# Four graph layers in one kernel: edge sums copied to a second half of the partitions, gate bias moved from products into bias columns

## The reference

```
# layer 1 (gated): means of neighbours, then a GRU cell
feat_in, feat_out = h @ W_in.T + b_in, h @ W_out.T + b_out
a  = concat(mean of feat_in[src] by dst, mean of feat_out[dst] by src)
gi, gh = a @ w_ih.T + b_ih, h @ w_hh.T + b_hh
r = sigmoid(i_r + h_r); z = sigmoid(i_z + h_z); n = tanh(i_n + r * h_n)
h = (1 - z) * n + z * h
# layer 2 (MLP): edge attributes summed per node
agg = segment_sum(edge_attr, col)                 # 3125 x 64
h = concat([x, agg, u[batch]])                    # 128 + 64 + 64 wide
h = leaky_relu(h @ w1 + b1); h = leaky_relu(h @ w2 + b2); out = h @ w3 + b3
```

## Time and profile before

| | |
|---|---|
| median of three runs | 860.36 us |
| profiled execution | 858.32 us, of which the span from first to last instruction is 856.6 us |
| busy share of the span | TensorE products 93%, weight loads 82%, DVE 71%, ACT 38%, GpSimd 3% |
| chain that ended last | PE 86%, DVE 8%, ACT 2%, issue 2%, DMA 1% |
| mean granted TensorE clock | 0.963 |

### The profile page before, as it was taken

How to read it: one execution, slowest core, us unless ns; L and a number is a source line. 1 busy time by engine, 2 the same in 40 slices (tenths; PEclk the granted TensorE clock), 3 DMA queues, 4 the chain that set the end, 5 groups by cost and what they waited for, 6 DMA issues and landing times.

```text
span 856.6 us, 16030 instructions
## 1 busy us (share of the span) xinstructions
PE 797.1 (93%) x6347; PEld 705.9 (82%) x6347; DVE 611.3 (71%) x970; ACT 324.6 (38%) x579; POOL 21.6 (3%) x39
## 2 busy tenths in 40 slices
PE   5699999999989999999989999979987999999995
PEld 2599999999979999789989996434546999699994
DVE  6998999999968777687876774657467455035654
ACT  0243444454556222522453332263325332432233
POOL 3500000000000000000000000000000000000000
PEclk9577999999998999999999999999999999999998
DMA  5455788888850000000000000000000000000001
GB/s 107 99 125 116 158 188 176 180 182 176 177 111 21 1 1 2 1 1 1 1 19 1 1 1 3 0 13 0 1 0 26 0 0 1 1 1 1 1 25 52
DMA packets 161175, 42.16 MB, mean 49 GB/s; under 512 B 155049, under 2 KB 159666, under 8 KB 161094
## 3 DMA queue, kind: packets, MB, share of 16 engines
q1 hardware_dynamic: 147882, 38.97, 20.3%
q10 hardware_dynamic: 11932, 0.81, 1.0%
q0 software_dynamic: 1280, 1.29, 0.6%
HBM read 39.04 MB, written 2.01 MB: 48 GB/s over the span
## 4 chain that ended last, share of the span: by engine, by line
PE 86%; DVE 8%; ACT 2%; issue 2%; DMA 1%; SPq 0%; POOL 0%; DVEq 0%; ACTq 0%
PE bank L1674 20%; PE bank L1675 19%; PE bank L1612 15%; PE bank L1602 10%; PE bank L1878 2%; PE bank L1810 2%; PE bank L1867 2%; PE bank L1866 1%; PE bank L1886 1%; PE bank L1736 1%; PE bank L1929 1%; PE bank L1930 1%; PE bank L1687 1%; DVE stage L1106 1%; PE bank L1814 1%
## 5 line engine op out<-in xcount | busy, mean ns | idle before, releaser
L1674 PE MATMUL bank<-stage,f_hi 125*128 125x392 f32 x1000 | 347.2, 347 | 3.8 <-issue 2.3
L1675 PE MATMUL bank<-stage,f_lo 125*128 125x392 f32 x1000 | 341.0, 341 | 0.0
L1106 DVE CAST stage<-counts 125x2352 fp32r<-125x2352 uint8 x120 | 164.2, 1380 | 77.0 <-PE bank L1675 76.9
L768 ACT ACTIVATE stage<-counts 125x1568 fp32r<-125x1568 uint8 x80 | 108.1, 1351 | 227.2 <-PE bank L1675 224.9
L1674 PEld LDWEIGHTS bank<-stage,f_hi 125*128 125x128 f32 x1000 | 188.7, 189 | 5.7 <-issue 4.0
L1675 PEld LDWEIGHTS bank<-stage,f_lo 125*128 125x128 f32 x1000 | 188.6, 189 | 0.6
L1612 PE MATMUL bank<-tmp,wb 128*65 128x25 f32 x2000 | 135.4, 223 | 0.2 <-DVE tmp L1064 0.2
L1612 PEld LDWEIGHTS bank<-tmp,wb 128*65 128x65 f32 x2000 | 132.1, 147 | 0.8 <-DVE tmp L1064 0.5
L722 ACT ACTIVATE counts<-bank 125x500 uint8<-125x500 f32 x188 | 87.9, 536 | 47.7 <-PE bank L1602 46.6
L1602 PE MATMUL bank<-rowb,xT 128*128 128x125 bf16 x1250 | 90.1, 230 | 10.0 <-DVE rowb L1042 5.3
L1039 DVE TENSOR_TENSOR xT<-xT,tmp 128x2560 bf16<-128x2560 bf16 (+1 forms) x63 | 92.8, 1473 | 2.5 <-PE bank L1602 2.4
(11 more groups left out here) (217 smaller groups left out, 674.8 us busy)
## 6 DMA issues: line engine op xcount, KB each, us to landing
wb<-in_edge_attr SPq DMA_DIRECT2D x125, 256.0 KB, 3.9
wa<-in_x SPq DMA_DIRECT2D x12, 125.0 KB
out<-wl SPq DMA_DIRECT2D x6, 250.0 KB
xT<-in_dst SPq DMA_DIRECT2D x63, 4.0 KB, 3.5
xT<-in_dst ACTq DMA_DIRECT2D x62, 4.0 KB, 3.2
wb<-in_L_gnn_w_ih SPq DMA_DIRECT2D x1, 384.0 KB, 3.4
gate_w_d<-wl SPq DMA_DIRECT2D x1, 384.0 KB, 4.2
counts<-in_dst SPq DMA_DIRECT2D x1, 360.9 KB
```

Source lines behind the costliest of these rows:

```text
L768: nc.scalar.activation(set_buffer(u, m), counts[:, SETS[u][0]:sum(SETS[u]), chunk(c)], ACT.Copy).then_inc(s["set_a_ready"], 1)
L1106: nc.vector.tensor_copy(set_buffer(u, m), counts[:, SETS[u][0]:sum(SETS[u]), chunk(pair * 2 + off)]).then_inc(s["set_d_ready"], 1)
L1674: mm(bank[h][:, 0:CH], f_hi[:, first + k, :], rhs[:, k, :], start=(first + k == 0), stop=False)
L1675: last = mm(bank[h][:, 0:CH], f_lo[:, first + k, :], rhs[:, k, :], start=False, stop=(first + k == HI - 1))
```

## The change

`hidden1` now issues the two products with `xT` first and then the two 64-row products, the second of which reads its weights (`l2w1b`) and its edge sums from partitions 64 to 127. Their copy is a DMA of `eaT[0:64]` to `eaT[64:128]` on SP's queue, and one more weight load puts the second half of the weight there. The bias of the gates is no longer a product: six products with one column each make `w_ih @ b` behind the weights' transposes, ACT copies the three columns to `cols`, and DVE adds them to the bias columns that sigmoid and tanh take. `has_edges` (L1327) goes; a node without an edge now sets the flag of the other branch, by two more DVE instructions in `all_looked`.

```
@@ sync
             sp.dma_start(gate_w_d, gate_w).then_inc(s["ws_out"], 16)
+            sp.dma_start(eaT[DE:2 * DE, :], eaT[0:DE, :]).then_inc(s["ea_twice"], 16)
             sp.wait_ge(s["y_made"], NC)
...
             sp.dma_start(l2w1a, p["L2_gnn_w1"][D:D + DE, :]).then_inc(s["l2w_in"], 16)
+            sp.dma_start(l2w1b, p["L2_gnn_w1"][D:D + DE, D:2 * D]).then_inc(s["l2w_in"], 16)
...
             sp.dma_start(l2w2, p["L2_gnn_w2"].rearrange("(k p) n -> p k n", k=2)).then_inc(s["l2w_in"], 16)
+            with sp.If(flag_of_odd(sp)):
+                sp.wait_ge(s["gates_done"], 4 * NC)
+                sp.dma_start(eaT[DE:2 * DE, :], eaT[0:DE, :]).then_inc(s["ea_twice"], 16)
@@ scalar
                 nc.scalar.activation(wl1[:, (3 + g) * D:(3 + g + n) * D], bank[k][:, 0:n * D], ACT.Copy).then_inc(s["fold_kept"], 1)
+            nc.scalar.activation(cols[:, C_BF:C_BF + 3], bank[1][:, FOLD_AT:FOLD_AT + 3], ACT.Copy).then_inc(s["fold_kept"], 1)
...
-                nc.scalar.activation(tmp[:, 3, :], tmp[:, 2, :], ACT.Tanh, bias=cols[:, C_BIH + 2:C_BIH + 3]).then_inc(s["gate_n"], 1)
+                nc.scalar.activation(tmp[:, 3, :], tmp[:, 2, :], ACT.Tanh, bias=cols[:, C_BN:C_BN + 1]).then_inc(s["gate_n"], 1)
@@ vector
             def all_looked():
+                nc.vector.tensor_reduce(g_most[:LO, :], dis_col[:, :], AX.X, ALU.min).then_inc(s["dve_w"], 1)
+                dve.wait_ge(s["dve_w"], landed.next())
+                nc.vector.tensor_scalar(unlike[:, 38:39], g_most[:LO, :], 0.0, None, ALU.is_le).then_inc(s["dve_w"], 1)
+                dve.wait_ge(s["dve_w"], landed.next())
...
-                if c == 1:
-                    nc.vector.tensor_scalar(has_edges, rowb[bias_rows, :], 0.0, None, ALU.is_gt).then_inc(s["ind_made"], 1)
...
+            dve.wait_ge(s["fold_kept"], 3)
             nc.vector.tensor_tensor(cols[:, C_BR:C_BZ + 1], cols[:, C_BIH:C_BIH + 2], cols[:, C_BHH:C_BHH + 2], ALU.add).then_inc(s["dve_w"], 1)
+            nc.vector.tensor_tensor(cols[:, C_BN:C_BN + 1], cols[:, C_BIH + 2:C_BIH + 3], cols[:, C_BF + 2:C_BF + 3], ALU.add)
+            dve.wait_ge(s["dve_w"], landed.next())
+            nc.vector.tensor_tensor(cols[:, C_BR:C_BZ + 1], cols[:, C_BR:C_BZ + 1], cols[:, C_BF:C_BF + 2], ALU.add).then_inc(s["dve_w"], 1)
             dve.wait_ge(s["dve_w"], landed.next())
@@ tensor
             pe.wait_ge(s["bias_w_made"], 1)
+            for g in range(3):
+                for k in range(2):
+                    mm(bank[1][:, FOLD_AT + g:FOLD_AT + g + 1], wt[f"wih{2 * g + k}"], cols[:, C_BIN + k:C_BIN + k + 1], start=(k == 0), stop=(k == 1))
...
             def input_gates(c, g, two_sums):
-                mm(bank[g][:, 0:CH], wt[f"wih{2 * g}"], wa[:, chunk(c)], start=True, stop=False)
+                last = mm(bank[g][:, 0:CH], wt[f"wih{2 * g}"], wa[:, chunk(c)], start=True, stop=not two_sums and g == 2)
...
                 if g < 2:
-                    mm(bank[g][:, 0:CH], wt[f"whh{g}"], xT[:, chunk(c)], start=False, stop=False)
-                mm(bank[g][:, 0:CH], bias_bf[:, g * D:(g + 1) * D], has_edges[:, chunk(c)], start=False, stop=True).then_inc(s["gates_done"], 1)
+                    last = mm(bank[g][:, 0:CH], wt[f"whh{g}"], xT[:, chunk(c)], start=False, stop=not two_sums)
+                if two_sums:
+                    last = mm(bank[g][:, 0:CH], bias_bf[:, g * D:(g + 1) * D], has_edges[:, chunk(c)], start=False, stop=True)
+                last.then_inc(s["gates_done"], 1)
...
             def inputs_there():
-                pe.wait_ge(s["ind_made"], 1)
...
             def hidden1(c):
                 for m in range(2):
                     mm(bank[m][:, 0:CH], l2w1x[:, m * D:(m + 1) * D], xT[:, chunk(c)], start=True, stop=False)
-                    last = mm(bank[m][:, 0:CH], l2w1a[:, m * D:(m + 1) * D], eaT[0:DE, chunk(c)], start=False, stop=True)
-                last.then_inc(s["l2_h1"], 1)
+                if c == 0:
+                    pe.wait_ge(s["ea_twice"], 16)
+                mm(bank[0][:, 0:CH], l2w1a[:, 0:D], eaT[0:DE, chunk(c)], start=False, stop=True)
+                mm(bank[1][:, 0:CH], l2w1b, eaT[DE:2 * DE, chunk(c)], start=False, stop=True).then_inc(s["l2_h1"], 1)
```

More of the change, by code:

```diff
@@ L92, in gnn_program @@
         mean_w = sb("mean_w", [D, 1], F32)
-        cols = sb("cols", [D, 28], F32)
+        cols = sb("cols", [D, 32], F32)
         wl1 = sb("wl1", [D, 12 * D], F32)
@@ L175, in gnn_program @@
         l2w1a = wl3[0:DE, 256:512]
+        l2w1b = wl3[DE:2 * DE, 256 + D:512]
         l2w1u = wl3[0:DE, 512:768]
@@ L194, in gnn_program @@
         C_BR, C_BZ, C_EPS = 19, 20, 21
+        C_BN, C_BF, FOLD_AT = 28, 29, 400
         C_BIN, C_BOUT, C_MIN, C_MOUT, C_MID, C_LOW = 22, 23, 24, 25, 26, 27
@@ L219, in gnn_program @@
             "l2w_in l2_bias l2_h1 l2_a1 l2_h2 l2_a2 l2_y l3_h l3_hk l3_y pad_made l3w_in rowb_sq bias_w_made bias_kept "
-            "bias_split fold_made fold_kept masks_made ind_made l2_b1 l2_b2 bu_made flag_part flag_made "
+            "bias_split ea_twice fold_made fold_kept masks_made l2_b1 l2_b2 bu_made flag_part flag_made "
             "g_table_made g_key_made g_hot g_used g_kept o_table_made o_key_made o_hot o_used o_kept deg_again g_idx_seen before_made before_summed next_in sqrt_made"
@@ L1395, in _ @@
             with dve.If(odd_kind):
+                dve.wait_ge(s["ea_twice"], 16)
                 nc.vector.tensor_scalar(edge_rows, rowb[bias_rows, :], cols[bias_rows, C_MIN:C_MIN + 1], None, ALU.mult).then_inc(s["odd_w"], 1)
@@ L1403, in _ @@
                 dve.wait_ge(s["odd_w"], 4)
-                nc.vector.tensor_scalar(has_edges, edge_rows, 0.0, None, ALU.is_gt).then_inc(s["odd_w"], 1)
+                nc.vector.tensor_scalar(has_edges, edge_rows, 0.0, None, ALU.is_gt)
+                nc.vector.tensor_copy(cols[:, C_BN:C_BN + 1], cols[:, C_BIH + 2:C_BIH + 3])
+                nc.vector.tensor_tensor(cols[:, C_BR:C_BZ + 1], cols[:, C_BIH:C_BIH + 2], cols[:, C_BHH:C_BHH + 2], ALU.add).then_inc(s["odd_w"], 1)
                 dve.wait_ge(s["odd_w"], 5)
@@ L1835, in gates @@
                     if c == 4:
-                        pe.wait_ge(s["l2w_in"], 64)
+                        pe.wait_ge(s["l2w_in"], 80)
                         for m in range(2):
@@ L1855, in _ @@
                 gates(True)
+                pe.wait_ge(s["ea_twice"], 32)
             with pe.Else():
@@ L1874, in hidden2 @@
                 else:
-                    pe.wait_ge(s["l2w_in"], 80)
+                    pe.wait_ge(s["l2w_in"], 96)
                 for m in range(2):
```

## The result

The changed kernel takes 851.05 us (median of 20 runs, 845.94 to 859.18), the kernel before 857.05 us (20 runs, 853.69 to 864.34). The ratio is 0.9922, 95% interval 0.9904 to 0.994: 6.7 us less, between 5.1 and 8.2. The forecast was 849.7, 8.6 us less than the profiled execution of before; the time lies in the range, and the gain is somewhat smaller than forecast.

A forecast was written before the change was run, and what follows sets the result against it. TensorE was taken to end nearly everything, with the ACT and DVE loop close behind in the gates. Gates -4.0, MLP -5.8, sum 1 -0.6, weights +1.8 make -8.6 us, from 858.3 to 849.7; range 843 to 858.

The forecast's parts named there:

- MLP: `hidden1`: two row-count changes go and one pass is shared, 0.73 us a round; -5.8 us, ends 3.2 and 8.5.
- weights: Before sum 0: six added one-column products cost +1.8 us, ends +1.5 and +2.9.
- gates: 24 bias products go, but only what the ACT and DVE loop waited for comes out: -4.0 us, ends 3.0 and 4.5.
- rival B: `hidden1`: a pair of 64-row products costs one product, -8.5 us in the MLP, total 847.0 us; chance 0.15.
- at full overlap some gain would stay in the wait for ACT and DVE: MLP: `result` can start about 2.3 us after `hidden2`, while a fully overlapped `hidden1` would take 2.2.
- Rival A: `hidden1`: the halves don't run together, only two row-count changes go, -3.2 us, total 852.3 us; chance 0.27.
- if the rise comes when it came before, L1643 runs behind it: Before sum 0: with the clock rising at its old time, L1643 runs at 0.13 us a pass, giving 1.4 us back.
- The last stretch: Gates, chunk 7: two bias products and two followers ahead of L1411 go, 0.9 us, of which about 0.7 is passed on.
- Rival D: Gates: new short idles of TensorE drop the clock to 1.2 GHz, +14 us there, total 867.7 us; chance 0.05.
- Rival C: Gates give nothing because the ACT and DVE loop refills what TensorE leaves; total 853.7 us; chance 0.08.
- Sum 1: Without the indicators on DVE, TensorE's wait of 0.63 us for a widening goes: -0.6 us.
- What cost nothing: The copy, extra weight load, small DVE instructions and SP's flag wait were forecast free, covered by idles or empty queues.

The follow-up runs named there:

- order and halves: The kernel before plus the edge sums' copy and the new `hidden1`, bias products kept: 848.70 us, ratio 0.9923.
- order alone: The changed kernel with both 64-row products of `hidden1` on rows 0 to 63, still neighbours in the queue: 853.14 us, ratio 0.9965.
- the bias alone: The changed kernel with the old `hidden1`, the copy still made but not read: 856.18 us, ratio 1.0.
- apart in the queue: The changed kernel with the two halves kept but `hidden1` ordered 128, 64, 128, 64 rows: one run, 865.66 us.

## Why the prediction was right, and where it was not

**The total was right, its split was not.** The range and the direction held. But the forecast's gain, 8.6 us, lies just beyond the interval of 5.1 to 8.2, and the three large terms were each off: MLP too small by 2.0 us, weights by 1.0, gates too large by 2.0. That the sum fits as well as it does is partly luck. The prediction held that only some 2% can be told from no change; with these runs 0.8% is clear of noise.

**MLP, the step that failed.** "The passes are issued as two of the first product, then two of the second", and so only one pass can be shared. The pass records say otherwise: the first passes of both products start 0.01 us apart, then the second passes together. So a pair costs one product, as rival B had it, and the step was mis-sized by a pass time (0.33 us) a round. The full overlap, 0.40 + 0.66 = 1.06 a round, is met: the starts of `hidden2` lie 6.75 us apart in after's second round, 7.80 in before's. The Trainium skill, "TensorE: Matmul & The Clock Gate", Part 3, has the span of packed products as one product's time plus some 4 ns for each further one; the trace agrees (0.86 for the pair, 0.85 for one), in fp32 with its two passes.

The forecast's remark that at full overlap some gain would stay in the wait for ACT and DVE is borne out in size. Eight rounds by 1.06 are 8.5; the stage gained 7.8. The two `hidden1` ahead of the first `hidden2` gave 7.96 - 5.89 = 2.07, and six rounds 47.21 - 41.48 = 5.73 instead of 6.36. The missing 0.6 is in the first round, which gave 0.64, and the sixth, 0.92. In the first, `result` waits for DVE's slope, where it did not before:

```profile
597.04 1.55 PE L1910 MATMUL bank<-tmp,wl 128*128 128x392 f32 x4 [0.33 <-DVE tmp L1456]
```

Rival A is out: order alone gave 3.0 us, order and halves 6.6. That the order is worth 0.40 a round was right.

**Weights, mis-sized.** +1.8 was said, ends 1.5 and 2.9; +2.8 was measured in after and +3.0 with the bias alone. The step that failed is "if the rise comes when it came before, L1643 runs behind it": I took a value near the lower end "since work is added ahead of the rise and not idle time". The rise did not come when it came before: 9.2 us behind the first transpose, not 6.1. The fold still ran at 0.50, so nothing was given back and the upper end was the right one. The same holds in three of the four other kernels with the six products ahead of the fold: rise at 9.5 to 10.9, stage 14.2 to 14.6. In the fourth (apart in the queue) the clock fell only behind the start of the transposes and the stage took 13.05, the forecast's +1.8. Behind the bias rows the same products cost 1.23 in the one execution there is: the price was the place more than the work. Why the rise comes later with the six products ahead is not shown.

**Gates, mis-sized twice.** The stretches up to the end of the long idle gave 2.64 of 3.3. Of the 0.67 missing, 0.22 is in chunks 1 and 2, where the loop takes 5.14 us from sigmoid to sigmoid, not 5.03: I had counted as TensorE's a part of the handovers that stays when DVE waits for ACT. Another 0.33 is behind chunk 5's sigmoid, where DVE's step to gate n (L1441) came 0.81 earlier and the scaled norm that ends the idle only 0.53. The last stretch, -0.7 forecast, came out at +0.68 in after and between -0.90 and +0.55 in the five other kernels with the long idle left (8.25 to 9.70 us). The two largest belong to the executions of 859.18 us (after) and 865.66 us (halves apart); the other four lie between -0.90 and +0.14. The prediction saw that "the idle grows" and priced the growth at nothing; it costs through the clock. With the idle filled the stretch is 7.8 in both kernels that do so, -1.3. So the sign of that step depends on how long TensorE stays at 1.2 GHz behind the idle: 3.2 us in before, 6.1 in after, 2.9 with the bias alone.

**Rival D** had the right resource in the wrong place. It put the fall into the short idles of chunks 2 to 5. There the clock stayed at 1.00, with idles of up to 0.99 us. The rule in the Trainium skill on D's side ("TensorE: Matmul & The Clock Gate", "A second HAM failure mode: psum-queue depth-cycling") is not borne out by these gates. **Rival C** is out as well: the gates gave at least 2.0 us.

**Sum 1.** The wait of 0.63 is gone, as said. The stage did not get shorter in the profiled execution, since the start of the gates waited 1.57 us for DVE instead of 1.16; in the seven other kernels with the bias columns that wait was 1.15 to 1.68, and the stage 177.3 to 178.4.

**What cost nothing** did cost nothing: the copy, the extra weight, the small DVE instructions and SP's wait show on no chain.

**Taken together,** the bias part is a draw: up to 1.0 us gained in sums 1 and 2 and 2.0 to 3.5 in the gates, 1.8 to 3.3 lost before sum 0. The new `hidden1` alone gave 6.6 us, the whole change 6.7.

**Open.** Why the low level behind the same idle lasts from 2.9 to 6.1 us was not settled; the traces show that the clock fell at different points of that idle, 1.9 to 4.5 us before its end. The Trainium skill, "TensorE: Matmul & The Clock Gate", Part 1, "What's actually happening", reports that the number of products at the low rate differs between runs of one kernel; these executions agree with that. The first 250 us, ahead of the change, differ by up to 13 us between the profiled executions, as much as the runs of after spread; what sets them was not studied.

## What to carry to other kernels

Two products of 64 rows cost as much as one, if they read different halves of the partitions and, writing different banks as here, stand next to each other in TensorE's queue; sort the products by row count first, which paid by itself (0.40 us a round here). Before a product is moved to a "free" place, look at the granted clock there: the same six small products cost 2.7 us ahead of the fold and 1.2 behind it. And when work is taken from an engine that is not the only bound, look at the idle that it leaves: where it is long, filling it with products that nobody reads brought the gates from 50.4 us (mean of six kernels) to 48.9 (mean of two).

## What was not expected of the hardware

- A product in fp32 is one instruction in the program and two passes in the trace, and the passes of two neighbouring products on different halves alternate: starts at 602.91, 602.92, 603.35 and 603.35 us.
- Twelve one-column passes took 2.72 us at 0.50, and the fold behind them still 2.77 at 0.50; where the fold stood first, the bias rows behind it took 1.54 (before) and 1.44 us, nearly all at 1.00, but 2.56 at 0.50 in the run without the six products.
- In the gates the clock stayed at 1.00 through idles of up to 1.57 us; in one of 6.64 us it fell, and it was 0.50 for 6.1 us behind it.
- The ten products in the idle ahead of the weights' transposes removed a low stretch that every other version has; the stage then took 10.1 us, 1.2 less than before the change.
